# Spreading each routing weight over 128 partitions: a DMA from a DRAM scratch in place of a product on TensorE

## What is computed

```
rw  = softmax over the active experts of normalize(h) @ normalize(sim) - sigmoid(gates)   # 16 weights a token
q,k,v = sum over e of rw[:, e] * (h @ Wqkv[e])          # 16 experts, 128 -> 3 x 64
attn  = causal softmax(q k^T / 8) @ v                   # 64 channels
out   = sum over e of (attn * rw[:, e]) @ Wo[e]         # 64 -> 128
x = x + 0.5 * out
```

## Time and profile before

| | us |
|---|---|
| median of three runs | 1756.37 (1755.73 to 1760.53) |
| the profiled execution | 1757.97 |
| its span in the profile | 1756.2 |
| first routed layer, about | 394 to 776 |
| second routed layer, about | 1373 to 1756 |

### The profile page before, as it was taken

One profiled execution on the slowest core, in us unless ns is written; L12 is line 12 of the kernel. 1 busy time (PEld: TensorE's weight loads), 2 busy tenths in 40 slices (PEclk: granted clock), 3 DMA queues, 4 the chain that ended last, 5 costly groups with the idle time before them and its releaser, 6 DMA issues.

```text
span 1756.2 us, 22310 instructions
## 1 busy us (share of the span) xinstructions
PE 1518.8 (86%) x7774; PEld 1098.1 (63%) x7774; DVE 1214.6 (69%) x2729; ACT 576.4 (33%) x1115; POOL 425.6 (24%) x368
## 2 busy tenths in 40 slices
PE   3988785996999999976888888878878699999997
PEld 3884454896899999952343333333323489999996
DVE  3666663666566666434999899898899656666653
ACT  2203443200221122114646556566464011212211
POOL 1130000000000000003666576566576000000000
PEclk9998996997999999987899989989998799999999
DMA  4000000000000000000000000000000000000000
GB/s 128 1 1 1 1 1 1 1 1 1 1 1 1 1 1 1 1 1 0 0 1 1 1 1 0 1 1 1 1 0 0 1 1 7 7 7 7 7 7 13
DMA packets 12206, 9.14 MB, mean 5 GB/s; under 512 B 2423, under 2 KB 11582, under 8 KB 11966
## 3 DMA queue, kind: packets, MB, share of 16 engines
q1 hardware_dynamic: 12094, 7.70, 1.5%
HBM read 5.60 MB, written 2.10 MB: 4 GB/s over the span
## 4 chain that ended last, share of the span: by engine, by line
PE 64%; DVE 15%; issue 13%; POOL 4%; ACT 4%; POOLq 0%; DVEq 0%; ACTq 0%
PE bank L1024 19%; PE bank L1027 7%; PE bank L881 5%; PE bank L1144 4%; PE bank L1012 3%; DVE hs L1503 3%; POOL both L500 3%; PE bank L917 2%; PE bank L974 2%; PE bank L959 2%; PE bank L1080 2%; DVE both L1495 2%; PE bank L956 2%; PE bank L1014 2%; PE bank L1139 2%
## 5 line engine op out<-in xcount | busy, mean ns | idle before, releaser
L1024 PE MATMUL bank<-wqkv_sb,xe 128*128 128x192 f32 x2048 | 381.8, 330 | 0.0
L1024 PEld LDWEIGHTS bank<-wqkv_sb,xe 128*128 128x128 f32 x2048 | 355.3, 193 | 17.1 <-issue 0.3
L1144 PE MATMUL bank<-both,ident 128*128 128x512 f32 x512 | 265.0, 619 | 3.0 <-DVE both L1495 3.0
L1440 DVE TENSOR_TENSOR xe<-xnT,bank 128x512 f32<-128x512 f32 x256 | 175.6, 687 | 106.4 <-PE bank L1012 103.9
L468 POOL TENSOR_TENSOR rstd<-ve,half_neg 128x4 f32<-128x4 f32 x32 | 32.3, 1008 | 796.6 <-DVE ve L1199 796.6
L753 ACT ACTIVATE bank<-dt,A 128x512 f32<-128x512 f32 x256 | 174.6, 687 | 145.7 <-DVE xe L1503 95.0
L500 POOL TENSOR_TENSOR both<-du,prob 128x512 f32<-128x512 f32 x128 | 161.9, 1271 | 101.2 <-DVE xe L1503 56.6
L500 POOL TENSOR_TENSOR both<-du,prT 128x512 f32<-128x512 f32 x128 | 161.8, 1273 | 55.9 <-DVE hs L1503 32.5
L1503 DVE TENSOR_TENSOR_SCAN xe<-bank,both 128x512 f32<-128x512 f32 x128 | 155.4, 1214 | 5.4 <-ACT bank L753 5.2
L1503 DVE TENSOR_TENSOR_SCAN hs<-bank,both 128x512 f32<-128x512 f32 x128 | 155.2, 1213 | 0.0
L1144 PEld LDWEIGHTS bank<-both,ident 128*128 128x128 f32 x512 | 98.1, 199 | 87.5 <-issue 54.6
(11 more groups left out here) (268 smaller groups left out, 2128.7 us busy)
## 6 DMA issues: line engine op xcount, KB each, us to landing
xs<-in_x_dram SPq DMA_DIRECT2D x8, 256.0 KB, 3.6
out_dram<-xs SPq DMA_DIRECT2D x8, 256.0 KB, 2.3
wqkv_sb<-in_wqkv_dram SPq DMA_DIRECT2D x1, 1536.0 KB
exp_sb<-in_expT_dram SPq DMA_DIRECT2D x1, 512.0 KB, 4.8
wo_sb<-in_wo_dram SPq DMA_DIRECT2D x1, 512.0 KB
win_sb<-in_W_in_dram SPq DMA_DIRECT2D x1, 256.0 KB
wout_sb<-in_W_out_dram SPq DMA_DIRECT2D x1, 128.0 KB
wq_sb<-in_WqT_dram SPq DMA_DIRECT2D x1, 64.0 KB
```

The lines of the kernel that those rows point to most:

```text
L1024: m = pe.matmul(bank[4 + j // 2][:, (j % 2) * 3 * HD:(j % 2 + 1) * 3 * HD], x_e, wqkv_sb[:, e, :], start=(e == 0 and j % 2 == 0), stop=(e ...
L1144: pe.matmul(bank[4 + k % NH][:], ident[:], hc[k % HRING], start=False, stop=(SUM_RANK[k] == sums_of(k // UNITS, k % NH))).then_inc(hc_used, 1)
L1440: dve.tensor_tensor(xe[i % RING][:], xnT[b % 2][:] if e < E2 else at2[:], bank[2 + i % 2][:], ALU.mult).then_inc(xe_made, 1)
```

## The change

TensorE's `spread` is gone from the routed layers. `wts` is turned as it is, in float32 (16 rows x 512), and ScalarE copies it to SBUF (`rows_sb`, two buffers). SP then writes the 16 rows (32 KB) to a scratch in DRAM, `w_rows`, waits until they have landed, and for each unit reads one row of 2 KB back with a stride of zero, which lays it on 128 partitions (256 KB written; for a pair unit two DMAs, 64 partitions each). There are eight destination buffers `wide` (the scan's `dt` and `du`, free in these layers), each with a semaphore. A buffer is filled again once the unit eight earlier has been scaled. SP's order is set by LOOK = 6: rows of units up to six clock steps ahead are asked for before the next step's other work. The three bf16 parts are no longer made. The stores of the result move into SP's new sequence.

```diff
+SLOTS = 8
+LOOK = 6
...
+        wide = [t[:, h, :] for t in dt_ + du for h in range(NH)]
+        w_rows = nc.dram_tensor("w_rows", [2 * NB, E2, L], F32).ap()
+        rows_sb = [t[0:E2, :] for t in (th, thr)]
...
+            def rows_to_dram(r, b):
+                sp.wait_ge(wT_sb, seen(2 * NB + r * NB + b + 1))
+                sp.dma_start(w_rows[r * NB + b], rows_sb[b % 2]).then_inc(rows_out, 16)
+
+            def widen(r, i):
+                n = r * NB * UNIT + i
+                b, e = divmod(clock_of(i), UNIT)
+                c = b if e < E2 else b - 1
+                if e == 0:
+                    sp.wait_ge(rows_out, 16 * (r * NB + c + 1))
+                if n >= SLOTS:
+                    sp.wait_ge(xe_made, seen(2 * FFN + n + 1 - SLOTS))
+                if e < E2:
+                    sp.dma_start(wide[n % SLOTS], w_rows[r * NB + c, e:e + 1, :].to_broadcast([P, L])).then_inc(wide_in[n % SLOTS], 16)
+                else:
+                    for k in range(2):
+                        row = NH * (e - E2) + k
+                        sp.dma_start(wide[n % SLOTS][k * HD:(k + 1) * HD, :], w_rows[r * NB + c, row:row + 1, :].to_broadcast([HD, L])).then_inc(wide_in[n % SLOTS], 16)
+
+            for r in range(2):
+                sent = 0
+                for u in CLOCK:
+                    if (u - 17) % UNIT == 0 and 0 <= (u - 17) // UNIT + 1 < NB:
+                        rows_to_dram(r, (u - 17) // UNIT + 1)
+                    while sent < NB * UNIT and clock_of(sent) <= u + LOOK:
+                        widen(r, sent)
+                        sent += 1
...
@@ ScalarE, routed front
-                    wT_copy(2 * NB + n, b % 3, pairs_at(r, b - 3) + PAIRS if b > 2 else experts_at(r, 0))
+                    act.wait_ge(wT_ps, seen(2 * NB + n + 1))
+                    if n > 1:
+                        act.wait_ge(rows_out, 16 * (n - 1))
+                    act.activation(rows_sb[b % 2], bank[1][0:E2, :], ACT.Copy).then_inc(wT_sb, 1)
@@ TensorE, routed front
-                    transpose3(w3, w3_made, seen(n + 1), wT_ps)
+                    pe.wait_ge(w3_made, seen(n + 1))
+                    for j in range(NT):
+                        m = pe.transpose(bank[1][0:E2, j * P:(j + 1) * P], wts[:, j, :], ident[:])
+                    m.then_inc(wT_ps, 1)
@@ TensorE, routed
-                def spread(i):
...
-                    while spreads < NB * UNIT and clock_of(spreads) <= u + AHEAD:
-                        spread(spreads)
-                        spreads += 1
@@ VectorE, routed
-                    three_parts(wts[:], rem[:], w3, E2, w3_made)
...
-                        dve.wait_ge(bc_ps, seen(base + i + 1))
+                        slot = (r * NB * UNIT + i) % SLOTS
+                        dve.wait_ge(wide_in[slot], 16 * wide_count(r, i))
                         dve.wait_ge(xe_used, seen(base + i + 1 - RING))
-                        dve.tensor_tensor(xe[i % RING][:], xnT[b % 2][:] if e < E2 else at2[:], bank[2 + i % 2][:], ALU.mult).then_inc(xe_made, 1)
+                        dve.tensor_tensor(xe[i % RING][:], xnT[b % 2][:] if e < E2 else at2[:], wide[slot], ALU.mult).then_inc(xe_made, 1)
```

More of the change, by code:

```diff
@@ L82, with wide_count @@
 CLOCK = range(-UNIT, UNIT * (NB + 1) + 8)
+SLOTS = 8
+LOOK = 6
+def wide_count(r, i):
+    n = r * NB * UNIT + i
+    return sum(1 if clock_of(m % (NB * UNIT)) % UNIT < E2 else 2 for m in range(n % SLOTS, n + 1, SLOTS))
 def due(gens, u):
@@ L334, in macaron @@
         stored = plain("stored")
+        rows_out = plain("rows_out")
+        wide_in = [plain(f"wide_in{i}") for i in range(SLOTS)]
         gvar_made, grstd_made, gnmr_made, gex_in, gex_out, gw3_made = (
@@ L418, in _, with store @@
                     sp.dma_start(dst, src).then_inc(w_in, 16)
-            for b in range(NB):
+            def store(b):
                 sp.wait_ge(acc_used, seen(5 * NB + b + 1))
                 sp.dma_start(outr[b], xs[:, b * L:(b + 1) * L].rearrange("p (j c) -> p j c", j=NT)).then_inc(stored, 16)
+            def rows_to_dram(r, b):
+                sp.wait_ge(wT_sb, seen(2 * NB + r * NB + b + 1))
+                sp.dma_start(w_rows[r * NB + b], rows_sb[b % 2]).then_inc(rows_out, 16)
+            def widen(r, i):
+                n = r * NB * UNIT + i
+                b, e = divmod(clock_of(i), UNIT)
[18 more added lines that the diff above has]
+                        sent += 1
+                    if r and (u - 4) % UNIT == 0 and 0 <= (u - 4) // UNIT - 2 < NB - 1:
+                        store((u - 4) // UNIT - 2)
+            store(NB - 1)
             sp.wait_ge(stored, 16 * NB)
@@ L559, in xT_copy @@
                 act.activation(xnT[par][:], bank[ps][:], ACT.Copy).then_inc(xT_sb, 1)
[L561 to L564, removed]
             def ffn(layer, r):
@@ L786, in logits @@
                 m.then_inc(lg_ps, 1)
[L788 to L794, removed]
             def ffn(layer, r):
@@ L1031, in routed @@
                 steps = by_clock(front, (5, 7, 17), back, (18, 20, 23, 26, 28, 29, 30, 31, 32, 33))
-                spreads = 0
                 for u in CLOCK:
                     i = unit_at(u)
-                    while spreads < NB * UNIT and clock_of(spreads) <= u + AHEAD:
-                        spread(spreads)
-                        spreads += 1
                     if i is not None:
@@ L1402, in front @@
                     dve.wait_ge(ex_out, seen(n + 1))
+                    dve.wait_ge(wT_ps, seen(2 * NB + n))
                     link(dve.tensor_tensor(wts[:], ex[:], eq[:], ALU.mult))
@@ L1405, in front @@
                     link(dve.reciprocal(den[:], den[:]))
-                    link(dve.tensor_tensor(wts[:], wts[:], over(den[:], E2), ALU.mult))
-                    yield
-                    dve.wait_ge(wT_ps, seen(2 * NB + n))
-                    three_parts(wts[:], rem[:], w3, E2, w3_made)
+                    dve.tensor_tensor(wts[:], wts[:], over(den[:], E2), ALU.mult).then_inc(w3_made, 1)
                     yield
@@ L1427, in back @@
                     yield
-                steps = by_clock(front, (0, 1, 3, 4, 10, 11, 12, 13, 15, 16), back, (22, 25, 28, 31, 37, 50))
+                steps = by_clock(front, (0, 1, 3, 4, 10, 11, 12, 13, 15), back, (22, 25, 28, 31, 37, 50))
                 for u in CLOCK:
```

## The result

The changed kernel takes 1779.6 us (median of 7 runs, 1768.8 to 1784.9) against 1756.7 (7 runs): ratio 1.012 (95% interval 1.009 to 1.015). It is slower by 1.2%, where 1694, faster by 3.6%, was forecast. The profiled execution takes 1779.6 us (span 1777.8).

What follows compares the result with a forecast made beforehand. TensorE was taken as the bound, paying every spread in full. A layer: -42.4 + 1.0 + 2.5 + 2 + 5 = -31.9 us, two layers -64, from 1758 to 1694 us; range 1670 to 1860.

Steps and rivals of the forecast that it cites:

- What goes: Spreads on TensorE in the routed layers: 42.4 us a layer saved, a steady period going from 43.0 to 37.7 us.
- What stays the same size: VectorE's product unchanged with its operand in SBUF; turning the weights in float32 for bf16 adds 1.0 us a layer.
- Six later changes: Later changes of sequence in a routed layer: 0.9 us of waiting each for write and first read, 5 us for six.
- Rival 4: Waits at changes of sequence lower TensorE's clock, 3.3 us at each of 12 later changes: 1734 us; chance 0.08.
- d: Time to lay one unit's 256 KB on SBUF in a full DMA queue: 1.46 us taken, ends 0.69 and 5.8.
- rivals 1 to 3: DMA engines mildly the bound, 0.20; one place serves 45 GB/s or two 90, 0.17; reads pay latency one by one, 0.03.
- Start of a layer: From first part to first scaled unit: parts and spread gone, 4.4 us of write and read come, +2.5 us.
- First change: First change of sequence in a routed layer, no pair units to fill it: new row comes later, +2 us (0 to 4).
- rival 1: DMA engines become the bound, mildly, at 1.7 to 2.1 us a unit: 1707 to 1860 us; chance 0.20.

Runs made afterwards that it cites:

- e4_free: Rows neither written nor waited for; SP reads rows of input W_in in their place, same read traffic, routing weights wrong (base kernel not stated): 1683.9 us, ratio 0.958.
- e3: Changed kernel with LOOK = 7 for 6 and ScalarE's copy of the weights one step earlier, together: 1706.9 us, ratio 0.970 to the kernel before.
- e6: e3 with three extra VectorE products (2.1 us, results unused) at the start of the scan: 1701.4 us, ratio 0.968 to the kernel before.
- e1: Changed kernel with LOOK = 7 for 6, so the last pair unit's read stands ahead of the write: 1738.9 us, ratio 0.989 to the kernel before.
- e2: Changed kernel with ScalarE copying the weights one step earlier, ahead of the copies of q and k: 1710.7 us, ratio 0.973 to the kernel before.
- e5: Changed kernel with seven extra TensorE products, results unused, ahead of each last pair unit: 1754.8 us, ratio 0.997 to the kernel before.

## Why the prediction was wrong

Against the 1694 of the forecast the profiled 1779.6 has 85.4 us more. By its own steps:

- **What goes** was right: 24 spreads take 5.29 us of TensorE in a period, for 5.28. But a period without any wait takes 38.27 (e4_free), not 37.7. **What stays the same size** was too low: the turning in float32 takes 0.44 us for 0.22, where 1.0 a layer was put for eight and it is 1.8, and the products of the 24 units take about 0.37 more than they did with spreads between them (the 16 expert units 21.1 for 20.8), which stood in no term. That is 0.58 a period, 4.6 us a layer, for 1.0.
- So it is luck in part that e3's routed layers, with SP holding nothing up, take 347.5 and 349.5 us where the forecast had 346.4 and 346.9: it had 5 us a layer for waits at later changes that e3 doesn't have, and lacked most of the 4.6. With the short scan the same code runs in 1699 us, less the 2.1 put in (e6).
- **Six later changes** is the step that failed. It reckoned the write against the first read behind it and put 0.9 us there. It said that "SP" holds "all later reads" behind the wait, but the write too is a waiting instruction, and behind *it* in SP's order stands a read of the sequence before. The order of SP's instructions, shown ahead of the prediction, has that read there. The wait falls one unit earlier than forecast, where TensorE has nothing else left to do, and is 3.1 us for 0.9. With the clock behind it a period is 6.0 us longer than e3's, and a layer 37 to 38 longer (2 to 3 of it at the first change), where the forecast put 5. e1 (order) and e2 (the time at which the write is free to go) each take it away: 41 and 69 us.
- The same step's size was low even at its own place: in e1, with the order that the step assumed, a period is 2.55 us longer than in e3, not 0.9, and a layer 20 us (first change included) for 5. Write and read take 1.56 and 3.47 (forecast 1.5 and 2.86), and VectorE then has the attention's maxima and the norm to do while TensorE waits.
- **Rival 4**, the clock, came true with the price that it had (3.3 a change; 3.0 by e5) and was given 0.08. It was held against it that the waits would be a third as long, as the step above had it, and that fell with the step; I treated the two as independent.
- **d**, said to be the one number on which all depends, was taken as 1.46. In the queue it is 0.64 to 0.94. For `bo` itself eight in a row land 1.65 us apart, near it, and a lone read took 3.1 to 3.2 us for 2.86, but rows of different units don't slow each other like that. The error was in the kernel's favour, and rivals 1 to 3, given 0.40 together, had no part in the result.
- **Start of a layer** +2.5 was about right: VectorE's first scaled unit stands 20.5 and 20.4 us behind the layer's start, for 17.3 and 17.4 before, +3.1. **First change** +2 was low: from VectorE's 16th product of the layer to its 17th went 7.9 and 7.8 us, and now 11.9 and 13.2, +4 and +5. In e3_both, with the earlier copy, it is 10.0 and 9.9, the +2 of the forecast. In the chain of the changed kernel, write and read are 4.75 us at the start and 4.69 at the first change, for 4.4:

```profile
408.86 1.64 DMA w_rows<-th
...
410.51 3.11 DMA dt<-w_rows
...
443.70 1.56 DMA w_rows<-thr
...
445.27 3.13 DMA dt<-w_rows
```

- **The scan**, 8.6 us, was in no term. The forecast took all code that isn't changed to keep its length.

The range, 1670 to 1860, holds the time, but for rival 1's sake, which had nothing to do with it.

## What to carry to other kernels

In a queue with in-order waits, cost every waiting instruction by all that stands behind it, back to work of an earlier stage that was ready; an instruction that waits late for its input should stand behind every issue that needs no wait. A wait can cost more than itself: 2.5 us of TensorE in one piece cost 6.0 a period, because the clock fell behind it, while 2.0 in two pieces (e1) cost 2.55, with the clock at 1.00 there. And moving a producer earlier helps only where the engines that do it have their inputs and the time there: one step on ScalarE brought 69 us, two on VectorE, with TensorE and ScalarE, cost 22.

## What the hardware showed that I had not expected

- A DMA that reads one DRAM row for 128 partitions has a price by the read: about 1.8 us each when the same row is asked for again and again, for 512 B and for 2 KB alike, but 0.64 to 0.94 us when eight different rows are in flight (up to 408 GB/s).
- Code that is not touched can change its length by 1.4%: the scan runs in 601 or in 609 to 611 us, each with its own pattern in which TensorE's clock falls, and 2.1 us of extra work at its start, counted in, moved it by -7.4 in one kernel and +11.5 in another.
- Seven useless products a sequence made a kernel 25 us faster (e5).
